# Key blocks of a fused attention kernel: where the query scales are made, and when the last weights are asked for

## The chip, the cores and the metric

One core of one Trainium2 chip. The metric is the device time of one launch in microseconds (us), as the median of several executions. The engines are TensorE (PE: matmuls and transposes; PEld: its weight loads), VectorE (DVE), ScalarE (ACT), GpSimd (POOL) and SyncE (SP, which here only issues DMAs). Each runs its own list of instructions in order and waits on semaphores for the others.

## The reference, cut to what matters

The whole block is attention with a paged cache, a second causal attention, a subject-dependent linear map and a feed-forward part with low-rank experts, for 64 sequences of 32 tokens. Only the head of the first attention bears on the change:

```
q = einsum('bsd,ed->bse', x, Wq)      # 32 heads of 128
k = einsum('bsd,ed->bse', x, Wk)      # 8 heads of 128
v = einsum('bsd,ed->bse', x, Wv)
q = rope(rmsnorm(q, q_norm_w), pos)   # rmsnorm: t * rsqrt(mean(t*t) + EPS) * w
k = rope(rmsnorm(k, k_norm_w), pos)
scores = einsum('bqhd,bkhd->bhqk', q, k_all) * SCALE
probs = softmax(where(valid, scores, -1e30))
```

`k_all` and `v_all` are the pages of a cache in front of the new keys and values. The kernel rotates queries without their norm and multiplies the scores by it later: it keeps the sums of squares of all queries and makes from them one table of **query scales** (`q_scale`), which the scores of the second stage need.

## The kernel before

Stage 1 (`stage1`) projects x with 12 blocks of weights of 512 columns: block 0 is the first half of V, blocks 1 to 8 are the queries, blocks 9 and 10 the keys, block 11 the second half of V. Every matrix is split in a high and a low part and every product is three fp32r matmuls. Stage 2 (`stage2`) is the attention over the cache; further stages follow. Between stage 1 and stage 2 stands a point that all engines must reach.

Stage 1 is written by hand, engine by engine. What follows is its key part, which runs over 16 **units** r = 0 to 15, eight for each block (`cb` = 0, 1; `u` = 0 to 7), each two tiles of 128 tokens.

- **PE** (`project`, `turn`): projections run two units ahead. In a loop it projects unit r + 2 and then transposes unit r (`turn`, L710). Unit n's projection waits until DVE has read the projection of unit n - 2 (`proj_free`), since there are two pairs of PSUM banks; `turn(r)` waits for `rotated`. After key unit 15 come the V units ("values"), the first two of them inside the same loop. From the third on they wait for `v_copied`.
- **ACT** (`k_block`): for each unit it squares the unit that has just been projected (`squares_of`, L370), takes the root of the sums (`root_of`, L377), copies what PE transposed into `turned` (`turn_copy`, L386), and in units 0 to 3 makes one quarter of the next weights' high part (`split`, L361). The two units ahead of the loop are done in front of it: squares of 0, squares of 1, then root of 0, root of 1. Behind unit 0's pieces stands `q_root` (L435), the root of all query sums, 512 columns.
- **DVE** (`rotate`, `norm`): for unit r two products with the sine and cosine tables (L585, L589; they free the banks), six small steps of the norm (L565 to L574), which need `root_of`, an addition (L596) and a multiplication by the norm (L600). In units 1 to 4 of a block a quarter of the weights' low part follows (L493). In the first block, behind units 2 to 7, stands one of six steps of `q_norm` each (L609 to L623, 512 columns), which turn `q_root` into the scales. The tiles `q_root`, `q_mean`, `q_inv` and `q_step` lie in the second quarter of `k_pool`, the place of the cache's keys, so that this quarter can't be loaded before they have been used.
- **POOL**: sixteen small copies from `q_inv` into `q_scale` (L327), then the loads of the first queries and keys of stage 2 (L70, L74), then a wait for the whole key pool and `gather_k` (L84, sixteen copies), which picks the pages of sequence 0.
- **SP** (`k_block`): asks for weights (`next_w`, L241; 1 MB), stores each unit's `turned` to `kT` (L273), and loads the key pool in 32 pieces of 256 KB (`load_pool`, L234). For the first block it asks for block 10's weights at its start, and loads two pieces behind each store. For the second block it first asks for block 11's weights, then waits for `q_scale_done` before the first store and loads two pieces behind the stores of units 1 to 4. Behind the stores of the first four V units (L248) stand two pieces each.

Of the kernel before, what the change touches and what calls it, by code (L numbers as in the profile page):

```python
# [28 lines left out]
ACT = mybir.ActivationFunctionType  # L29
# [6 lines left out]
D, HQ, HK = 128, 32, 8  # L36
G = HQ // HK
# [4 lines left out]
SEQ = P // S  # L42
NT = 4
# [46 lines left out]
def stage1(nc, c, a, scratch):  # L90

    UN = TILES // 2
    VU = UN
    RU = 2 * UN
    QM = HK * NT * G
    QN = HK * NT
    POOL_PIECES = 8
    with ExitStack() as opened:  # L98
        hold = opened.enter_context

        k_pool = c["k_pool"]
# [84 lines left out]
        pos_f = early[:, 1152:1152 + TILES]  # L186
        NQ = HK * TILES * G
        q_sums = sums[:, 0:HK, :].rearrange("p h n -> p (h n)")
        q_root = k_pool[:, quarter:quarter + NQ]
        q_mean = k_pool[:, quarter + NQ:quarter + 2 * NQ]  # L190
        q_inv = k_pool[:, quarter + 2 * NQ:quarter + 3 * NQ]
        q_step = k_pool[:, quarter + 3 * NQ:quarter + 4 * NQ]

        @block.sync
        def _(sp):
# [33 lines left out]
            def load_pool(part, piece, pieces):  # L229

                size = quarter // pieces
                first = part * quarter + piece * size
                cols = slice(first, first + size)
                sp.dma_start(k_pool[:, cols], a["kpool"][:, cols]).then_inc(c["pool_loaded"], 16)  # L234

            def next_w(blk):
                if isinstance(blk, int) and blk == 0:
                    sp.wait_ge(w_lo_piece, KC)
                else:
                    sp.wait_ge(w_lo_done, blk)  # L240
                sp.dma_start(w_raw[:, :], a["w1"][bass.ds(blk + 1, 1)].rearrange("o p n -> p (o n)")).then_inc(w_loaded, 16)  # L241
# [16 lines left out]

            def k_block(cb):

                next_w(9 + cb)
                if cb == 0:
                    for k in range(2):
                        sp.wait_ge(q_store_free[k], 16 + 16 * HK * NT // 2)
                    sp.wait_ge(q_sums_done, QN + 2)
                else:
                    sp.wait_ge(q_scale_done, SEQ * G)
                for u in range(UN):
                    b0 = u * 2 * SEQ
                    sp.wait_ge(turned_done, cb * UN + u + 3)  # L270
                    src = turned[:, u % 2, :].rearrange("p (b n) -> p b n", n=GS)
                    dst = scratch["kT"][b0:b0 + 2 * SEQ, :, cb, :].rearrange("b p n -> p b n")
                    sp.dma_start(dst, src).then_inc(store_free[u % 2], 16)  # L273
                    if cb == 0:
                        for k in range(2):
                            load_pool(u // 4 * 3, u % 4 * 2 + k, POOL_PIECES)
                    elif 1 <= u <= 4:
                        for k in range(2):
                            load_pool(1, 2 * u - 2 + k, POOL_PIECES)

            next_w(0)
            for u in range(UN):
# [16 lines left out]
        @block.gpsimd  # L299
        def _(pool):  # L300

            pool.memset(c["ident"][:, :], 0.0).then_inc(ident_step, 1)
            for s in range(SEQ):
                pool.wait_ge(ident_step, s + 1)
                pool.iota(c["tok_i"][s * S:(s + 1) * S, :], pattern=[[0, 1]], base=0, channel_multiplier=1).then_inc(ident_step, 1)
            pool.wait_ge(ident_step, SEQ + 1)
            pool.iota(key_i[:, :], pattern=[[1, L]], base=0, channel_multiplier=0).then_inc(ident_step, 1)
            pool.wait_ge(ident_step, SEQ + 2)
            pool.affine_select(out=c["ident"][:, :], in_=c["ident"][:, :], compare_op=ALU.not_equal, fill=1.0,
                               base=0, pattern=[[-1, P]], channel_multiplier=1).then_inc(ident_step, 1)  # L310
            pool.memset(ones[:, :], 1.0).then_inc(ident_step, 1)

            pool.sem_inc(q_sums_kept, 1)
            kept = q_sums.rearrange("p (h b) -> p h b", h=HK)
            with pool.Fori(0, 4) as i:
                for cb in range(2):
                    for span in range(NT):
                        pool.wait_ge(q_sums_turned, (i * 2 + cb) * NT + span + 1)
                        pool.tensor_copy(kept[:, bass.ds(i * 2 + cb, 1), span * BS:(span + 1) * BS].rearrange("p o b -> p (o b)"),
                                         sums_rows.rearrange("p (b s) -> p b s", s=S)[:, :, 0]).then_inc(q_sums_kept, 1)  # L320

            pool.wait_ge(q_inv_done, 1)
            inv4 = q_inv.rearrange("p (e h b) -> p h e b", e=2, h=SEQ)
            scale4 = c["q_scale"][:, :, :].rearrange("p b (e g) -> p g e b", g=G)
            for g in range(G):
                for q in range(SEQ):
                    pool.tensor_copy(scale4[q * S:(q + 1) * S, g, :, :], inv4[g * S:(g + 1) * S, q, :, :]).then_inc(q_scale_done, 1)  # L327

            pool.wait_ge(turn_done, RU + 2)
            pool.wait_ge(store_free[0], 16 + 16 * (VU + (RU - UN) // 2 + 1))  # L330
            for k in range(2):
                pool.wait_ge(q_store_free[k], 16 + 16 * HK * NT // 2)
            c["load_q"](pool, 0, 0)
            c["load_k_own"](pool, 0, 0)
            c["load_q"](pool, 1, 1)
            pool.wait_ge(c["pool_loaded"], 16 * 4 * POOL_PIECES)
            c["gather_k"](pool, 0, 0)

        @block.scalar
        def _(act):  # L340
# [48 lines left out]
            def v_copy(n, u, stores):  # L389

                act.wait_ge(proj_done, n + 1)
                act.wait_ge(store_free[u % 2], stores * 16 + 16)
                for t in range(2):
                    m = act.activation(turned[:, u % 2, t * 512:(t + 1) * 512], ps_proj[:, u % 2, t, :], ACT.Copy)
                m.then_inc(v_copied, 1)
# [25 lines left out]
            def k_block(cb):  # L421
                for u in range(UN):
                    r = cb * UN + u
                    ahead = cb + (u + 2) // UN
                    if not (cb == 1 and u >= UN - 2):
                        squares_of(r + 2, HK + ahead, (u + 2) % UN)
                        root_of(ahead, (u + 2) % UN)
                    if r == 0:
                        act.wait_ge(q_sums_kept, QN + 1)
                    turn_copy(r, VU + cb * (UN // 2) + u // 2, u)  # L430
                    if u < KC:
                        split(cb, 10 + cb, u)
                    if r == 0:
                        act.wait_ge(q_rotated, QM + 2)
                        act.activation(q_root, q_sums, ACT.Sqrt, bias=eps[:, 0:1], scale=1.0 / D).then_inc(q_root_done, 1)  # L435

            x_high_piece(0)
            for q in range(KC):
# [20 lines left out]
                    q_block(i, cb)  # L459
            for u in range(2):  # L460
                squares_of(u, HK, u)
            for u in range(2):
                root_of(0, u)
            for cb in range(2):
                k_block(cb)
            for u in range(UN):
                v_copy(VU + RU + u, u, VU + RU // 2 + u // 2 * 2)

        @block.vector
        def _(dve):  # L470
# [134 lines left out]
            def q_norm(k):  # L605

                if k == 0:
                    dve.wait_ge(q_root_done, 1)
                    dve.tensor_scalar(q_mean, q_sums, 1.0 / D, EPS, ALU.mult, ALU.add).then_inc(q_inv_step, 1)  # L609
                elif k == 1:  # L610
                    dve.reciprocal(q_inv, q_root).then_inc(q_inv_step, 1)
                elif k == 2:
                    dve.wait_ge(q_inv_step, 2)
                    dve.tensor_tensor(q_step, q_inv, q_inv, ALU.mult).then_inc(q_inv_step, 1)
                elif k == 3:
                    dve.wait_ge(q_inv_step, 3)
                    dve.tensor_tensor(q_step, q_step, q_mean, ALU.mult).then_inc(q_inv_step, 1)
                elif k == 4:
                    dve.wait_ge(q_inv_step, 4)
                    dve.tensor_scalar(q_step, q_step, 0.5 * SCALE, -1.5 * SCALE, ALU.mult, ALU.add).then_inc(q_inv_step, 1)  # L620
                elif k == 5:
                    dve.wait_ge(q_inv_step, 5)
                    dve.tensor_tensor(q_inv, q_step, q_inv, ALU.mult).then_inc(q_inv_done, 1)  # L623
# [40 lines left out]
            for cb in range(2):  # L664
                for u in range(UN):
                    rotate(cb * UN + u, u, tab_k, (cb, u))
                    if 1 <= u <= KC:
                        split(10 + cb, cb, u - 1)
                    if cb == 0 and 2 <= u:
                        q_norm(u - 2)  # L670

        @block.tensor
        def _(pe):
# [1350 lines left out]
```

## Time and profile before

| | us |
|---|---|
| median of 3 runs | 3061.29 |
| lowest, highest | 3060.76, 3063.66 |
| the profiled execution | 3071.46 |
| its span, from first to last instruction | 3069.9 |
| PE busy in the span | 3027.6 (99%) |
| DVE, ACT, POOL busy | 1860.2, 1543.4, 595.0 |

The profiled execution is 10.2 us longer than the median of the runs. Times within the trace are microseconds from the start of its span. On the time line a row gives start, duration, engine, line of the kernel, operation, what is written and read, how often, and in brackets how long the engine stood idle before it and what released it. Matmuls overlap, so a matmul's duration is longer than its distance to the next.

### The profile page before, as it was taken

The numbers are of one execution on the slowest core, as the hardware profiler recorded it, in microseconds if no ns is written. First come the engines' busy times: TensorE is split into PE (matmuls) and PEld (weight loads), VectorE is DVE, ScalarE is ACT, GpSimd is POOL, SyncE is SP. The second block draws the span as 40 slices with busy tenths as digits, with TensorE's granted clock in tenths as the row PEclk, the third lists the DMA queues.
The fourth block names the chain that finished last, engine by engine and source line by source line (L and its number), as shares of the span: only waits on it lengthen the run. The fifth ranks groups of instructions, "written<-read, shape, count | busy, mean of one in ns | idle before, by whom it ended". The sixth has DMA issues, their size and how long they took to land.

```text
span 3069.9 us, 91713 instructions
## 1 busy us (share of the span) xinstructions
PE 3027.6 (99%) x36256; PEld 2351.8 (77%) x36256; DVE 1860.2 (61%) x3587; ACT 1543.4 (50%) x2949; POOL 595.0 (19%) x1430
## 2 busy tenths in 40 slices
PE   8999998999999999999999999999999999999999
PEld 7777777767777777777777888888888888888887
DVE  6777768477888877888886444442333333544445
ACT  6666655377777777777776222221333333322221
POOL 0000001055455455455452000000000000200000
PEclk9999999999999999999999999999999999999999
DMA  5333334566676676676677344412333333743311
GB/s 167 97 110 105 115 110 131 166 208 205 211 220 204 206 219 206 210 220 205 209 219 229 110 126 125 124 65 100 104 103 104 97 110 100 240 148 110 109 41 55
DMA packets 508661, 456.02 MB, mean 149 GB/s; under 512 B 33985, under 2 KB 470593, under 8 KB 503746
## 3 DMA queue, kind: packets, MB, share of 16 engines
q1 hardware_dynamic: 475010, 362.80, 39.3%
q0 software_dynamic: 33344, 88.46, 8.9%
q8 instruction: 273, 4.47, 0.6%
q14 instruction: 34, 0.28, 0.0%
HBM read 321.03 MB, written 130.02 MB: 147 GB/s over the span
## 4 chain that ended last, share of the span: by engine, by line
PE 78%; DMA 1%; issue 0%; DVE 0%; ACT 0%; DVEq 0%; SPq 0%
PE ps_o L1009 18%; PE ps_scores L993 16%; PE s_ps L58 8%; PE s_ps L60 8%; PE s_ps L59 8%; PE s_ps_proj L58 5%; PE s_ps_proj L59 5%; PE s_ps_proj L60 5%; PE s_ps_o L1542 1%; PE s_ps_scores L1518 1%; PE yv_ps L60 1%; PE yv_ps L59 1%; PE yv_ps L58 1%; PE s_ps L1717 0%; PE s_ps L1708 0%
## 5 line engine op out<-in xcount | busy, mean ns | idle before, releaser
L1009 PEld LDWEIGHTS ps_o<-weights_t,v_all 32*128 32x128 f32 x17408 | 514.0, 187 | 111.1 <-issue 110.3
L1009 PE MATMUL ps_o<-weights_t,v_all 32*128 32x128 f32 x17408 | 564.4, 277 | 5.6 <-issue 3.7
L993 PE MATMUL ps_scores<-k_slot,q_slot 128*32 128x288 f32 (+1 forms) x8192 | 525.9, 397 | 7.0 <-PEq L98 4.8
L898 ACT ACTIVATE probs<-masked,shift 128x544 f32<-128x544 f32 x512 | 382.9, 748 | 248.1 <-DVE shift L944 246.6
L944 DVE CUSTOM_DVE_ANT_0 masked<-ps_scores,reach,scale_now 128x544 f32<-128x544 f32 x512 | 390.2, 762 | 179.2 <-PE ps_scores L993 175.0
L993 PEld LDWEIGHTS ps_scores<-k_slot,q_slot 128*32 128x32 f32 x8192 | 241.2, 110 | 201.6 <-issue 9.6
L957 DVE STREAM_TRANSPOSE weights_t<-probs 128x544 f32<-128x544 f32 x512 | 376.8, 736 | 23.5 <-ACT probs L903 10.3
L903 ACT ACTIVATE probs<-probs,inv 128x544 f32<-128x544 f32 x512 | 375.7, 734 | 0.0
L1101 ACT ACTIVATE s_h_hi<-s_h_raw 128x2048 fp32r<-128x2048 f32 x64 | 122.8, 1919 | 488.2 <-PE s_ps L60 472.3
L84 POOL COPY k_slot<-k_pool 128x256 f32 x1024 | 359.3, 410 | 34.8 <-DMA k_pool<-kpool_in 19.1
L58 PE MATMUL s_ps_proj<-y_hi,s_w_hi 128*128 128x512 f32 x640 | 253.1, 395 | 0.0
L59 PE MATMUL s_ps_proj<-y_lo,s_w_hi 128*128 128x512 f32 x640 | 250.0, 391 | 0.0
L60 PE MATMUL s_ps_proj<-y_hi,s_w_lo 128*128 128x512 f32 x640 | 249.1, 389 | 0.0
L58 PE MATMUL ps_proj<-x_hi,w_hi 128*128 128x512 f32 x512 | 202.9, 396 | 0.0
L414 ACT ACTIVATE turning<-ps_proj 64x512 f32<-64x512 f32 x256 | 151.8, 593 | 99.6 <-PE ps_proj L60 97.3
L58 PE MATMUL s_ps<-s_w_hi,s_h_hi 128*128 128x512 f32 x512 | 199.5, 390 | 1.4 <-DVE s_h_lo L1128 1.4
L60 PE MATMUL ps_proj<-x_hi,w_lo 128*128 128x512 f32 x512 | 199.4, 390 | 0.0
L58 PE MATMUL s_ps<-s_h_hi,s_w_hi 128*128 128x512 f32 x512 | 199.4, 389 | 0.0
L59 PE MATMUL ps_proj<-x_lo,w_hi 128*128 128x512 f32 x512 | 199.3, 389 | 0.0
L59 PE MATMUL s_ps<-s_w_lo,s_h_hi 128*128 128x512 f32 x512 | 199.2, 389 | 0.0
L60 PE MATMUL s_ps<-s_h_hi,s_w_lo 128*128 128x512 f32 x512 | 199.2, 389 | 0.0
L60 PE MATMUL s_ps<-s_w_hi,s_h_lo 128*128 128x512 f32 x512 | 199.2, 389 | 0.0
(201 smaller groups left out, 4723.0 us busy)
## 6 DMA issues: line engine op xcount, KB each, us to landing
v_all<-vpool_in SPq DMA_DIRECT2D x1024, 128.0 KB, 3.0
qT_scratch<-k_pool SPq DMA_DIRECT2D x32, 1024.0 KB, 5.1
q_slot<-qT_scratch POOLq DMA_DIRECT2D x64, 512.0 KB, 3.5
oT_scratch<-o_t POOLq DMA_DIRECT2D x128, 256.0 KB, 5.1
s_h_raw<-oT_scratch SPq DMA_DIRECT2D x32, 1024.0 KB, 5.8
aT_scratch<-s_o_t SPq DMA_DIRECT2D x32, 1024.0 KB, 5.7
s_h_raw<-aT_scratch SPq DMA_DIRECT2D x32, 1024.0 KB
w_raw<-w_in SPq DMA_DIRECT2D x11, 1024.0 KB, 8.0
```

The costliest lines, as they stand in the source:

```text
L58: pe.matmul(out, a_hi, b_hi, start=start, stop=False)
L59: pe.matmul(out, a_hi, b_lo, start=False, stop=False)
L60: return pe.matmul(out, a_lo, b_hi, start=False, stop=stop)
L84: m = pool.tensor_copy(k_slots[slot][:, first + k, :], k_pool[:, bass.ds(page[k], 1), :].rearrange("p o n -> p (o n)"))
L414: act.activation(swapped[g][to, :], bank[g][of, :], ACT.Copy)
L898: act.activation(probs[:, k % BUF, :], masked[:, k % 2, :], ACT.Exp, bias=shift[:, k % BUF:k % BUF + 1], scale=-1.0, accum_out=total[:, k ...
L903: act.activation(probs[:, k % BUF, :], probs[:, k % BUF, :], ACT.Copy, scale=inv[:, k % BUF:k % BUF + 1]).then_inc(w_done, 1)
L944: dve.tensor_tensor_reduce(masked[:, k % 2, :], ps_scores[:, k % 2, LOW:LOW + KEYS], reach[:, k // HK, :], scale_now[:, k // HK, k % HK:k ...
L957: dve.transpose(weights_t[:, k // G % 4, k % G, :], probs[:, k % BUF, :]).then_inc(turned_w, 1)
L993: m = pe.matmul(ps_scores[q * S:(q + 1) * S, k % 2, cols], q_slots[j][:, head, r * S:(r + 1) * S], k_slots[j][:, pages, head * PSIZE:(head ...
L1009: m = pe.matmul(ps_o[:, q, 0:GS], v_all[rows, j, t, e * D:(e + 1) * D], weights_t[rows, g, :, t * S:(t + 1) * S], start=t == 0, stop=t == NPP)
L1101: act.activation(h_hi[k % 2][:, :, :].rearrange("p g (b s) -> p b g s", s=S), h_raw[k % 2][:, :, :].rearrange("p b (g s) -> p b g s", s=S) ...
```

## The change

Four things are altered, all in stage 1.

1. ACT takes the root of key unit 0 right behind its squares, ahead of the squares of unit 1.
2. The query scales are made later. `q_root` moves on ACT from behind key unit 0 to behind the second V unit's copy, the six `q_norm` steps on DVE from between the key units to behind all of them, and the sixteen copies on POOL from ahead of the three first loads of stage 2 to behind them. The four tiles move from `k_pool` into `by_cos` and `by_sin`, the rotation's tiles, which are not used any more by then. A wait for the copies is added before `gather_k`.
3. SP asks for block 11's weights behind the sixth store of the first key block and its two pieces, where before it did so behind the eighth. SP no longer waits for the scales.
4. The second quarter of the key pool is loaded in the second key block one piece behind each of the eight stores, where before it was two pieces behind stores 1 to 4.

```
-        q_root = k_pool[:, quarter:quarter + NQ]
...
+        q_root, q_mean = by_cos[:, 0:NQ], by_cos[:, NQ:2 * NQ]
+        q_inv, q_step = by_sin[:, 0:NQ], by_sin[:, NQ:2 * NQ]
...
             def k_block(cb):
 
-                next_w(9 + cb)
                 if cb == 0:
+                    next_w(9)
...
-                else:
-                    sp.wait_ge(q_scale_done, SEQ * G)
...
                             load_pool(u // 4 * 3, u % 4 * 2 + k, POOL_PIECES)
-                    elif 1 <= u <= 4:
-                        for k in range(2):
-                            load_pool(1, 2 * u - 2 + k, POOL_PIECES)
+                        if u == 5:
+                            next_w(10)
+                    else:
+                        load_pool(1, u, POOL_PIECES)
...
+            pool.wait_ge(q_inv_done, 1)
...
+                    pool.tensor_copy(scale4[q * S:(q + 1) * S, g, :, :], inv4[g * S:(g + 1) * S, q, :, :]).then_inc(q_scale_done, 1)
+
+            pool.wait_ge(q_scale_done, SEQ * G)
             pool.wait_ge(c["pool_loaded"], 16 * 4 * POOL_PIECES)
             c["gather_k"](pool, 0, 0)
...
             for u in range(2):
                 squares_of(u, HK, u)
-            for u in range(2):
                 root_of(0, u)
...
                 v_copy(VU + RU + u, u, VU + RU // 2 + u // 2 * 2)
+                if u == 1:
+                    act.wait_ge(rotated, RU + 1)
+                    act.activation(q_root, q_sums, ACT.Sqrt, bias=eps[:, 0:1], scale=1.0 / D).then_inc(q_root_done, 1)
...
-                    if cb == 0 and 2 <= u:
-                        q_norm(u - 2)
+            for k in range(UN - 2):
+                q_norm(k)
```

**ACT, at the head of the key units** (`squares` x8 is one unit; `k_pool<-sums,eps` is `q_root`). Before:

```order
L370 ACTIVATE squares,sums<-ps_proj 128x128 x16
L377 ACT_TABLE_LOAD
L377 ACTIVATE root<-sums,eps 128x8 x2
L370 ACTIVATE squares,sums<-ps_proj 128x128 x8
L377 ACTIVATE root<-sums,eps 128x8
L386 ACTIVATE turned<-ps_turn 128x4x4x32 x2
L361 ACTIVATE w_hi<-w_raw 128x512
L435 ACTIVATE k_pool<-sums,eps 128x512
```

Now:

```order
L368 ACTIVATE squares,sums<-ps_proj 128x128 x8
L375 ACT_TABLE_LOAD
L375 ACTIVATE root<-sums,eps 128x8
L368 ACTIVATE squares,sums<-ps_proj 128x128 x8
L375 ACTIVATE root<-sums,eps 128x8
L368 ACTIVATE squares,sums<-ps_proj 128x128 x8
L375 ACTIVATE root<-sums,eps 128x8
L384 ACTIVATE turned<-ps_turn 128x4x4x32 x2
L359 ACTIVATE w_hi<-w_raw 128x512
```

The table load and the first root stand between the squares of unit 0 and of unit 1, and `q_root` is gone from here.

**DVE, from the end of key unit 4 to the products of unit 5** (L611 is the longest of the six `q_norm` steps). Before:

```order
L596 TENSOR_TENSOR turning<-by_cos,by_sin 128x1024
L600 TENSOR_TENSOR turning<-turning,nw 128x1024
L493 TENSOR_TENSOR w_lo<-w_raw,w_hi 128x512
L611 RECIPROCAL k_pool<-k_pool 128x512
L585 TENSOR_TENSOR by_cos<-ps_proj,k_pool 128x1024
L589 TENSOR_TENSOR by_sin<-ps_proj,k_pool 128x8x64 x2
```

Now, behind the last key unit:

```order
L597 TENSOR_TENSOR turning<-turning,nw 128x1024
L606 TENSOR_SCALAR by_cos<-sums 128x512
L608 RECIPROCAL by_sin<-by_cos 128x512
L611 TENSOR_TENSOR by_sin<-by_sin 128x512
L614 TENSOR_TENSOR by_sin<-by_sin,by_cos 128x512
L617 TENSOR_SCALAR by_sin<-by_sin 128x512
L620 TENSOR_TENSOR by_sin<-by_sin 128x512
L98 UNCONDITIONAL_BRANCH
```

All six steps stand in a row there, and nothing but the end of the stage follows.

**SP, from the last stores of the first key block into the second** (`kT_scratch` is a unit's store, `k_pool<-kpool_in` a piece of the pool). Before, from the store of unit 7:

```order
L273 DMA kT_scratch<-turned 128x8x128 [waits turned_done]
L234 DMA k_pool<-kpool_in 128x512 x2
L241 DMA w_raw<-w_in 128x2048 [waits w_lo_done]
L273 DMA kT_scratch<-turned 128x8x128 [waits turned_done,q_scale_done]
L273 DMA kT_scratch<-turned 128x8x128 [waits turned_done]
L234 DMA k_pool<-kpool_in 128x512 x2
```

Now, from the store of unit 5:

```order
L269 DMA kT_scratch<-turned 128x8x128 [waits turned_done]
L232 DMA k_pool<-kpool_in 128x512 x2
L239 DMA w_raw<-w_in 128x2048 [waits w_lo_done]
L269 DMA kT_scratch<-turned 128x8x128 [waits turned_done]
L232 DMA k_pool<-kpool_in 128x512 x2
L269 DMA kT_scratch<-turned 128x8x128 [waits turned_done]
L232 DMA k_pool<-kpool_in 128x512 x2
L269 DMA kT_scratch<-turned 128x8x128 [waits turned_done]
L232 DMA k_pool<-kpool_in 128x512
```

The request for the weights stands two stores earlier, and every store of the second block has one piece behind it.

## Rows read from the trace of the kernel before

**Rows 1.** Busy us (x instructions) by stretch, granted clock, DMA share, GB/s
```profile
463.02:575.87 112.85, 102.75 (x481) 84.70 (x481) 98.37 (x181) 54.17 (x277) 8.50 (x16) 0.94 0.46 136
617.10:3069.90 2452.80, 2437.99 (x33536) 1894.62 (x33536) 1442.13 (x2903) 1193.65 (x2152) 562.27 (x1350) 1.00 0.51 154
```
**Rows 2.** Time line of PE: transposes (L710), first matmuls behind a gap
```profile
465.26 1.97 PE L710 MATMUL ps_turn<-ident,turning 128*128 128x128 f32 x8 [2.08 <-DVE turning L600]
475.34 1.03 PE L710 MATMUL ps_turn<-ident,turning 128*128 128x128 f32 x8
488.56 1.04 PE L710 MATMUL ps_turn<-ident,turning 128*128 128x128 f32 x8
492.62 0.79 PE L58 MATMUL ps_proj<-w_hi,x_hi 128*128 128x512 f32 x1 [3.03 <-DVE by_sin L589]
499.77 1.03 PE L710 MATMUL ps_turn<-ident,turning 128*128 128x128 f32 x8
531.46 1.03 PE L710 MATMUL ps_turn<-ident,turning 128*128 128x128 f32 x8
536.70 0.61 PE L58 MATMUL ps_proj<-w_hi,x_hi 128*128 128x512 f32 x1 [4.20 <-DVE by_sin L589]
575.87 1.03 PE L710 MATMUL ps_turn<-ident,turning 128*128 128x128 f32 x8
579.06 0.50 PE L58 MATMUL ps_proj<-w_hi,x_hi 128*128 128x512 f32 x1 [2.15 <-ACT turned L394]
617.12 5.24 PE L993 MATMUL ps_scores<-k_slot,q_slot 128*32 128x288 f32 x44 [4.75 <-PEq L98]
```
**Rows 3.** Time line of ACT, 453 to 585 us
```profile
453.04 0.25 ACT L370 ACTIVATION_READ_ACCUMULATOR squares<-ps_proj 128x1 f32 x1
459.97 1.28 ACT L377 ACT_TABLE_LOAD   x1
461.27 0.49 ACT L377 ACTIVATE root<-sums,eps 128x8 f32<-128x8 f32 x2
492.12 0.63 ACT L361 ACTIVATE w_hi<-w_raw 128x512 fp32r<-128x512 f32 x1
532.96 0.63 ACT L361 ACTIVATE w_hi<-w_raw 128x512 fp32r<-128x512 f32 x1 [4.16 <-DMA w_raw<-w_in]
583.69 1.09 ACT L394 ACTIVATE turned<-ps_proj 128x512 f32<-128x512 f32 x2 [4.68 <-DMA kT_scratch<-turned]
```
**Rows 4.** Time line of DVE, 461 to 562 us
```profile
461.60 0.17 DVE L565 TENSOR_SCALAR nw<-sums 128x8 f32<-128x8 f32 x1 [5.81 <-ACT root L377]
486.95 3.35 DVE L611 RECIPROCAL k_pool<-k_pool 128x512 f32<-128x512 f32 x1
534.23 1.22 DVE L585 TENSOR_TENSOR by_cos<-ps_proj,k_pool 128x1024 f32<-128x1024 f32 x1
548.69 1.22 DVE L585 TENSOR_TENSOR by_cos<-ps_proj,k_pool 128x1024 f32<-128x1024 f32 x1
555.14 1.22 DVE L585 TENSOR_TENSOR by_cos<-ps_proj,k_pool 128x1024 f32<-128x1024 f32 x1
561.17 1.23 DVE L585 TENSOR_TENSOR by_cos<-ps_proj,k_pool 128x1024 f32<-128x1024 f32 x1
```
**Rows 5.** SP's time line; then us to landing, stores issued at 528.9, 553.9, 571.7
```profile
524.74 0.47 SPq L241 DMA_DIRECT2D w_raw<-w_in  x1
...
kT_scratch<-turned SPq DMA_DIRECT2D x1, 512.0 KB, 5.6
...
kT_scratch<-turned SPq DMA_DIRECT2D x1, 512.0 KB, 3.5
...
kT_scratch<-turned SPq DMA_DIRECT2D x1, 512.0 KB, 3.2
```
**Rows 6.** Time line of POOL: the scale copies, and the first gather
```profile
516.41 9.37 POOL L327 COPY q_scale<-k_pool 32x128 f32<-32x128 f32 x16 [63.18 <-DVE k_pool L623]
598.18 5.54 POOL L84 COPY k_slot<-k_pool 128x256 f32 x16 [19.09 <-DMA k_pool<-kpool_in]
```

More of the change, by code:

```diff
@@ L188, in stage1 @@
         q_sums = sums[:, 0:HK, :].rearrange("p h n -> p (h n)")
-        q_root = k_pool[:, quarter:quarter + NQ]
-        q_mean = k_pool[:, quarter + NQ:quarter + 2 * NQ]
-        q_inv = k_pool[:, quarter + 2 * NQ:quarter + 3 * NQ]
-        q_step = k_pool[:, quarter + 3 * NQ:quarter + 4 * NQ]
+        q_root, q_mean = by_cos[:, 0:NQ], by_cos[:, NQ:2 * NQ]
+        q_inv, q_step = by_sin[:, 0:NQ], by_sin[:, NQ:2 * NQ]
         @block.sync
@@ L320, in _ @@
                                          sums_rows.rearrange("p (b s) -> p b s", s=S)[:, :, 0]).then_inc(q_sums_kept, 1)
[L322 to L327, printed above, removed]
             pool.wait_ge(turn_done, RU + 2)
@@ L335, in _ @@
             c["load_q"](pool, 1, 1)
+            pool.wait_ge(q_inv_done, 1)
+            inv4 = q_inv.rearrange("p (e h b) -> p h e b", e=2, h=SEQ)
+            scale4 = c["q_scale"][:, :, :].rearrange("p b (e g) -> p g e b", g=G)
+            for g in range(G):
+                for q in range(SEQ):
+                    pool.tensor_copy(scale4[q * S:(q + 1) * S, g, :, :], inv4[g * S:(g + 1) * S, q, :, :]).then_inc(q_scale_done, 1)
+            pool.wait_ge(q_scale_done, SEQ * G)
             pool.wait_ge(c["pool_loaded"], 16 * 4 * POOL_PIECES)
@@ L432, in k_block @@
                         split(cb, 10 + cb, u)
-                    if r == 0:
-                        act.wait_ge(q_rotated, QM + 2)
-                        act.activation(q_root, q_sums, ACT.Sqrt, bias=eps[:, 0:1], scale=1.0 / D).then_inc(q_root_done, 1)
             x_high_piece(0)
```

## The prediction

> **What bounds the kernel now.** I read the busy time by stretch first, then PE's time line, then those of the engines that PE waits for. Stage 2 and all that follows is PE at work for 2437.99 of 2452.80 us at a granted clock of 1.00 [rows 1]; nothing in the change reaches there. The key units are another matter: in their 112.85 us PE is busy for 102.75, DVE for 98.37, and the granted clock is 0.94 [rows 1]. So the reading is of this stretch alone, and of the 41 us behind it up to the start of stage 2 at 617.12 [rows 2].
>
> PE's rhythm there is one projection and one group of eight transposes per unit. Undisturbed, that period is 6.34 us: from the transposes of unit 4 at 499.77 to those of unit 9 at 531.46 it is 31.69 us for five [rows 2]. Every departure from it is a loss. PE stands ready for the transposes of unit 0 at 463.2 (465.26 less the idle 2.08), and starts those of unit 15 at 575.87 [rows 2]. That is 112.7 us for fifteen periods, which undisturbed are 95.1. **17.6 us are lost**, in three places [rows 2]:
> - Units 0 and 1: 2.1 us of idle time before unit 0's transposes, and 475.34 - 465.26 - 6.34 = 3.7. The eight transposes take 1.97 us, where those of later units take 1.03: TensorE is at its lower clock (1.2 of 2.4 GHz) behind the wait. Together 5.8.
> - Units 1 to 4: 488.56 - 475.34 - 2 x 6.34 = 0.5, and 499.77 - 488.56 - 6.34 = 4.9, with an idle 3.03 before the projection at 492.62 whose first matmul is 0.79 long; the clock is down again. Together 5.4.
> - Units 9 to 15: 575.87 - 531.46 - 6 x 6.34 = 6.4, with an idle 4.20 before the projection at 536.70.
>
> **Part 1, the first root.** DVE stands idle for 5.81 us until 461.60, because the root of unit 0 waits behind unit 1's squares [rows 4]. ACT had unit 0's squares at 453.29 and then waited for unit 1's projection; the table load of 1.28 us and both roots (0.49) come at 459.97 [rows 3]. Now table load and root stand at 453.3 and are done by about 455.3, which is ahead of unit 1's squares: nothing on ACT comes later. Unit 0 was turned at 465.26, 3.7 us behind the norm's start at 461.60; the norm now starts when DVE has done the products, 5.8 us sooner (461.60 less 5.81), so unit 0 is rotated near 459.5, ahead of 463.2, when PE is ready. The idle 2.1 goes, with it the low clock. Unit 1's products can start at 460.0 (its squares are done just before the table load of 459.97 [rows 3]) and free the banks 2.47 us later: the products at 534.23 let PE start at 536.70 [rows 2, 4]. That is 462.5, in time. All 5.8 us go.
>
> **Part 2, the scales out of the key units.** The reciprocal alone keeps DVE for 3.35 us right before the products of unit 5, for which PE waits [rows 4]. Without the six steps DVE's period is 6.03 us (555.14 to 561.17), or 6.45 with a piece of the weights' low part (548.69 to 555.14) [rows 4]. The first is under PE's 6.34. The second is over it by 0.11, and occurs at four units of each block. So the 5.4 us go, but DVE becomes what is late next, narrowly. A piece of the high part on ACT ends at 492.12 + 0.63, that is 4.19 us behind the transposes at 488.56 [rows 2, 3]. With 0.6 for the low part and 2.47 for the products, PE is free to go on 7.3 us behind them; by its own rhythm it wants to go on at 6.34 + 0.9 = 7.24, where 0.9 is 6.34 less the 5.4 us of a projection. That is 0.1 us for the first piece and 0.1 for each of the next three, 0.4 per block, **0.8 us back**. The bounds are 0 (DVE's slack absorbs it, as it does partly in the last six periods) and 2.
>
> Where the six steps and the copies go there must be cover. `q_root` can run when the second V unit has been copied: 583.69 + 1.09 [rows 3], shifted by the gain to about 568.3. None of the rows has it in that place; two copies of the same 512 columns take 1.09, which bounds it. ACT then has its next unit to wait for, and PE's next is two units behind. On DVE the reciprocal is 3.35, and each of the other five steps is at most 1.23, the price of 1024 columns [rows 4]: 9.5 at most. The sixteen copies are 9.37 and the gather 5.54 [rows 6]. So the chain ends by 568.3 + 1.1 + 9.5 + 9.4 + 5.5 = 593.8 at the latest. Stage 2 starts at 617.12 less the gain, 600.6. **The chain has 6.8 us to spare and costs nothing.** Before it was the last piece of the pool that started the gather at 598.18 [rows 6]; that piece is now at 581.7, ahead of the copies' end.
>
> **Part 3, the last weights.** ACT waits 4.16 us for the weights of block 11 until 532.96 and DVE and PE behind it [rows 2, 3]; they had been asked for at 524.74 [rows 5], 8.2 us earlier. Now the request stands two stores earlier. In the new rhythm unit 5 is turned at 463.2 + 0.4 + 31.7 = 495.3, its store follows about 3.7 us later (ACT squares unit 7 in between), two pieces follow, and the request is out at 501.5: the weights land at 509.7. ACT wants them 3.56 us (492.12 - 488.56) behind the transposes of unit 8, at 518. The wait goes with 8 us in hand, and with it 6.1 us of the 6.4; the other 0.3 is DVE's lateness, counted above.
>
> The request now stands ahead of unit 6's store. That store has a twin: the one at 528.9 was issued 4.1 us behind such a request and took 5.6 us to land, against 3.5 with two pieces behind it and no such load ahead [rows 5]. Its buffer is wanted again two units later, 11 us after the issue. It costs nothing. The Trainium skill ("DMA: Bandwidth & Descriptors", section "Queues, rings and completion order") says that the increment of a DMA's semaphore lands only after every earlier write from the same SDMA engine, across queues. This speaks against the new place, and the 5.6 us agree with it. By the rule the store lands no sooner than the weights, some 4 us after its issue, and the sum is the same.
>
> **Part 4, one piece per unit.** SP has time: in the key units a piece is asked for in under a microsecond and a unit lasts 6.34. The one place where it can hurt is behind unit 15's store, where there was no piece. ACT's second V copy waits for that store, until 583.69, and PE's fourth V projection waits for the copy [rows 3]. A store with nothing behind it landed in 3.2 us, one with two pieces in 3.5 [rows 5]: **0.3 us back**. The upper bound is 2.4 (5.6 less 3.2), if the piece acts as the 1 MB load did; nothing suggests a gain. I take 0.3, since a piece behind a store is what the 3.5 shows.
>
> **The sum.** 5.8 + 5.4 + 6.4 = 17.6 gained, 0.8 + 0.3 given back: 16.5 us. The profiled execution of 3071.46 us would take 3055.0, its span 3053.4 instead of 3069.9. The median of the runs is 10.2 us under the profiled one; the gain is taken off it whole: 3061.29 - 16.5 = **3044.8 us**, 0.54% less.
>
> **Rivals.**
> - *The V units give some of it back.* The third waits 2.15 us for ACT, as before [rows 2]. The additional piece delays the stores behind it, on which ACT's next two copies wait; at its upper bound that is 2.4 us, and if TensorE falls to its lower clock in the longer wait, the following unit takes 7.15 us (492.62 to 499.77) instead of 5.4 [rows 2], 1.8 more. The gain is 12.6 to 15, the time near 3048. Against it: the first matmul behind the 2.15 is only 0.50 long, not 0.79 [rows 2], so the clock held there. The Trainium skill ("TensorE: Matmul & The Clock Gate", section "What's actually happening") calls the throttled clock the default, which activity lifts; the wait of 2.08 that ended at 465.26 was followed by the lower clock and that of 2.15 was not [rows 2], so the trace bears the rule out at one of two waits of like length, and by the rule a wait that was harmless before need not stay so. 0.14.
> - *The last weights still hold up a unit,* because load and stores hamper each other more than the twin shows. It decides from 8 us of further delay, and gives the 6.1 us back: 3050.9. 0.06.
> - *The scales' chain ends stage 1, and the kernel is slower.* The chain from `q_root` to the end of the gather is 25.5 us in series at its bounds, at the very end of the stage, where before only the gather stood. It sets the start of stage 2 from 6.8 us over that price on, and makes the kernel slower from 6.8 + 16.5 = 23.3 us on, that is if steps on DVE and POOL took about twice as long there. At two and a third times the price the time is near 3072. For it speaks that POOL's durations are rough; against it that DVE has nothing else to do then, and that the 9.37 us were measured beside a busy DVE. Late but not slower 0.03, slower 0.03.
> - *The change doesn't do what it says:* other waits stand right behind those removed, and the time is within 6 us of the old. Nothing in the rhythm of units 4 to 9 shows one. 0.02.
>
> **How the numbers follow.** The forecast has a chance of 0.72; with the others that is 1. About 0.2% (6 us) is what a measurement of this kernel can tell from no change. Faster by more: 0.72 + 0.14 + 0.06 + 0.03 = 0.95; same 0.02; slower 0.03. The range: at the best neither the 0.8 nor the 0.3 is given back, 3043.7, and runs spread by a microsecond or two, so 3042. Upwards it takes in DVE's bound and the V units' case to 12.6 (3048.7) and the same spread: 3050.
>
> **What would show it.** In the changed trace: the transposes of unit 0 near 463.2 and 1.03 long; those of unit 15 near 559 and no idle time over 0.3 on PE between; DVE never over 1 us idle up to unit 8; the third V unit still waiting about 2.1; ACT's second V copy at 567.3; the scale copies on POOL over by 589, the gather by 594, both ahead of PE's last V matmul near 595; stage 2 from 600.6. A wait for weights near 518, a first V matmul of 0.79, or a stage 2 that starts right behind the gather would each show its rival right. The sum would be wrong if the period of 6.34 us did not hold for fifteen units in a row: DVE would then be at a wait that the gaps of before had hidden.

## The result

| | us |
|---|---|
| before, median of 6 runs | 3061.38 (3060.76 to 3065.18) |
| changed, median of 6 runs | 3048.30 (3045.06 to 3052.43) |
| ratio | 0.9955 (0.9945 to 0.9965) |
| the changed kernel's profiled execution | 3048.38, span 3046.8 |

The ratio is the changed kernel's time over that of the kernel before in the same comparison, with its 95% interval in brackets. The change makes the kernel 13.1 us faster, where 16.5 were forecast. 16.5 us are a ratio of 0.9946, inside the interval, near its lower end. The changed kernel's runs lie on about 3045, 3048 and 3052; the profiled execution is a middle one. The trace of before that the prediction used was a long one: 3071.46 where its median is 3061.

The stretches of the changed kernel, us (from:to, length, busy PE, PEld, DVE, ACT, POOL, granted clock, DMA share, GB/s):

```profile
463.02:559.30 96.28, 96.28 (x484) 80.36 (x482) 87.09 (x166) 53.48 (x276) 0.00 (x0) 1.00 0.53 156
559.30:600.00 40.70, 33.89 (x151) 27.38 (x149) 6.24 (x8) 10.35 (x20) 14.14 (x35) 0.99 0.60 204
600.00:3046.80 2446.80, 2433.48 (x33536) 1891.27 (x33536) 1445.70 (x2904) 1193.29 (x2152) 561.56 (x1350) 1.00 0.51 155
```

The key units, 112.85 us in [rows 1], now take 96.28, with PE busy for all of them and the clock at 1.00. PE's time line there, with the start of stage 2:

```profile
462.87 1.04 PE L707 MATMUL ps_turn<-ident,turning 128*128 128x128 f32 x8
469.23 1.03 PE L707 MATMUL ps_turn<-ident,turning 128*128 128x128 f32 x8
475.75 1.03 PE L707 MATMUL ps_turn<-ident,turning 128*128 128x128 f32 x8
...
520.43 1.03 PE L707 MATMUL ps_turn<-ident,turning 128*128 128x128 f32 x8
527.01 1.03 PE L707 MATMUL ps_turn<-ident,turning 128*128 128x128 f32 x8
...
559.01 1.03 PE L707 MATMUL ps_turn<-ident,turning 128*128 128x128 f32 x8
562.20 0.50 PE L58 MATMUL ps_proj<-w_hi,x_hi 128*128 128x512 f32 x1 [2.15 <-ACT turned L392]
600.05 7.88 PE L990 MATMUL ps_scores<-k_slot,q_slot 128*32 128x288 f32 x80 [4.71 <-PEq L98]
```

Against [rows 2] the idle times of 2.08, 3.03 and 4.20 are gone, the 2.15 in the V units stays. From unit 0 to unit 15, fifteen periods, it takes 96.1 us. Stage 2 starts at 600.05 instead of 617.12, **17.07 us** sooner. The next rows are ACT's first root, and its later `q_root` with the copies around that:

```profile
453.14 1.28 ACT L375 ACT_TABLE_LOAD   x1
454.44 0.30 ACT L375 ACTIVATE root<-sums,eps 128x8 f32<-128x8 f32 x1
...
566.72 1.08 ACT L392 ACTIVATE turned<-ps_proj 128x512 f32<-128x512 f32 x2 [4.57 <-DMA kT_scratch<-turned]
567.69 0.72 ACT L464 ACTIVATE by_cos<-sums,eps 128x512 f32<-128x512 f32 x1
570.32 1.09 ACT L392 ACTIVATE turned<-ps_proj 128x512 f32<-128x512 f32 x2 [1.91 <-DMA v_pages_scratch<-turned]
```

And the scales' chain on DVE (its first and last step) and POOL:

```profile
568.44 0.43 DVE L606 TENSOR_SCALAR by_cos<-sums 128x512 f32<-128x512 f32 x1 [12.16 <-ACT by_cos L464]
...
574.08 0.69 DVE L620 TENSOR_TENSOR by_sin<-by_sin 128x512 f32<-128x512 f32 x1
...
574.84 7.60 POOL L331 COPY q_scale<-by_sin 32x128 f32<-32x128 f32 x16 [12.60 <-DVE by_sin L620]
583.44 5.54 POOL L84 COPY k_slot<-k_pool 128x256 f32 x16 [1.00 <-POOL q_scale L331]
```

The chain is over at 588.98, 11.1 us ahead of stage 2. So the trace puts 17 us into stage 1, the timed runs show 13, and the two profiled spans differ by 23.1. The experiments had to say which of these is the change's.

### The profile page after: what moved, and what is told of

Same layout as the page of the kernel before. It is cut to its first block, busy times and chain, and to the rows that moved or that the text cites. A ratio compares the mean times of both kernels' runs of the same rounds, so it can differ in the third digit from the quotient of the medians.

```text
span 3046.8 us, 91713 instructions
## 1 busy us (share of the span) xinstructions
PE 3016.6 (99%) x36256; PEld 2344.2 (77%) x36256; DVE 1863.7 (61%) x3587; ACT 1543.1 (51%) x2949; POOL 592.6 (19%) x1430
## 4 chain that ended last, share of the span: by engine, by line
PE 79%; issue 0%; DVE 0%; ACT 0%; DMA 0%; DVEq 0%
PE ps_o L1006 18%; PE ps_scores L990 16%; PE s_ps L58 8%; PE s_ps L60 8%; PE s_ps L59 8%; PE s_ps_proj L58 5%; PE s_ps_proj L59 5%; PE s_ps_proj L60 5%; PE s_ps_o L1539 1%; PE s_ps_scores L1515 1%; PE yv_ps L60 1%; PE yv_ps L59 1%; PE yv_ps L58 1%; PE s_ps L1714 0%; PE s_ps L1705 0%
```

## The experiments

Each is the kernel before or the changed one with one edit, or with none. The kernel before was run beside them each time, and every ratio is against it. Where two ratios are set against each other below, they come from the same comparison, unless it is said otherwise. 0.001 of the time is 3.1 us.

**The kernel before again.** No edit.

> The kernel before, unchanged, to see how much of a launch's time is not set by the code. The trace of before spans 3069.9 us, its timed runs lie near 3061; the trace of after spans 3046.8 and its timed runs fall on 3045, 3048 and 3052. Theory A: the key units are the same in every execution (unit 0 turned at 465.3, unit 15 at 575.9, stage 2 from 617.1), and what differs lies behind 617, above all at the end of stage 2, where the trace of before has 98 matmuls in 5.91 us at the lower clock and that of after in 3.16. Then the span here is 3060 to 3070 with stage 2 from 617. Theory B: the low clock in the key units is itself a matter of the execution, and stage 2 starts up to 4 us earlier here than in the first trace.

Measured: 3061.68 (10 runs; ratio 1.0001, 0.9989 to 1.0012), profiled span 3060.2. Stage 2 started at 615.1, not 617.1, so there is truth in theory B. From there to the start of the third stage it took 1057.0 us against 1063.0 in the first trace, as theory A has it. Both scatter. In stage 1 the two executions differ most at the gap for the last weights; unit 0 and the period behind it are 0.3 and 0.6 us later here. The projection behind the gap, in the first trace and in this one:

```profile
536.70:543.86 7.16, 7.16 (x24) 5.69 (x25) 6.85 (x17) 0.77 (x2) 0.00 (x0) 0.76 0.50 146
```
```profile
536.35:541.93 5.58, 5.58 (x24) 4.56 (x25) 5.38 (x11) 0.78 (x2) 0.00 (x0) 1.00 0.63 188
```

Here the same 24 matmuls ran at a granted clock of 1.00 behind a gap of 3.02, and the load landed in 7.0 us, not 8.2. The period from unit 9 to unit 10 was 9.65 instead of 12.40: over the undisturbed 6.34, this loss is 3.3 us in one execution and 6.1 in another.

**Only the first root.**

```
-            for u in range(2):
                 root_of(0, u)
```

> Only the first root is moved (part 1). The prediction's sum gives it 5.8 us: the idle 2.1 before unit 0's transposes and the 3.7 behind it go, the later losses stay at 5.4 and 6.4. Stage 2 from 611.3, time 0.9981 of before. Rival: the time comes back at the next wait (DVE's six steps and the wait for weights absorb it), and stage 2 starts within 1 us of 617.1.

Measured: 3055.21 (10 runs), ratio 0.9982 (0.9970 to 0.9994), as expected. In its trace unit 9 is turned at 526.39, 5.9 us ahead of the kernel before in the run above (532.28). But stage 2 starts at 612.7, only 2.4 ahead, because the gap for the weights was 4.00 long, with the low clock behind it:

```profile
531.43:539.50 8.07, 8.07 (x25) 6.35 (x26) 7.69 (x19) 0.79 (x2) 0.00 (x0) 0.67 0.44 130
```

Unit 10 came 13.11 us behind unit 9, a loss of 6.8, the largest in any trace. The traced execution was a long one, 3061.52. Against the first trace it starts stage 2 4.4 us sooner, so the rival, less than 1 us, is not met either way; the ten timed runs carry the verdict.

**Only the scales.** The edit is part 2 of the change with the SP wait gone, and nothing else.

> Only the query scales are moved (part 2), with the wait of SP for them gone; first root, request for the last weights and pairs of pieces as before. The sum gives 5.4 us less: stage 2 from 611.7, time 0.9982 of before. The transposes of unit 4 come 13.2 us, not 18.6, ahead of those of unit 6 less the periods. Rival: the gap at unit 4 was due to the lateness carried over from units 0 and 1, and only part of the 5.4 goes.

Measured: 3058.75 (10 runs), ratio 0.9991 (0.9981 to 1.0001), half of what was expected and not clear of nothing. In the trace the step is as forecast: units 2, 3 and 4 are 6.58 and 6.39 us apart, where in the repeated run of before they are 6.88 and 11.22. The rival, that this loss was carried over from units 0 and 1, falls: those are as late here as ever (10.98 us apart). Again the period at the later gap is longer than in the repeated run of before (11.62 against 9.65), and stage 2 starts at 612.7.

**Only the last weights.**

```
-                next_w(9 + cb)
...
+                        if u == 5:
+                            next_w(10)
```

> Only the request for the last weights is moved behind the sixth store (part 3). The sum gives 6.1 us less: the idle 4.20 before the projection at 536.70 goes and with it the low clock behind it; stage 2 from 611.0, time 0.9980 of before. Rival: less than 4 us, if in some executions of before the clock doesn't fall in that gap.

Measured: 3058.22 (10 runs), ratio 0.9988 (0.9978 to 0.9998). The period at the gap is 6.57 and stage 2 starts at 611.7, 3.4 us sooner than in the repeated run of before and 5.4 sooner than in the first. The timed gain is 3 to 4 us, the rival's, and its condition was met in the repeated run of before. The interval, 0.6 to 6.7 us, does not exclude the 6.1. Added up, the three single edits bring 12.0 us timed.

**The changed kernel again.** No edit.

> The changed kernel, unchanged, to see which part of its 13 us in the timed runs is fixed and which varies. Theory: stage 1 has no clock lottery left, so the transposes of units 0 and 15 and the start of stage 2 fall within 0.5 us of 462.9, 559.0 and 600.05 of its first trace, while stage 2 and behind scatter by several us as in before. Against before, whose stage 2 started at 617.1 and 615.1 in two traces, that is 15 to 17 us; ratio 0.9945 to 0.996. Rival: stage 2 itself has become longer by 2 to 4 us, which would show in its span (1063.0 and 1057.0 in before, 1058.5 in after).

Measured: 3047.05 (6 runs), ratio 0.9943 (0.9929 to 0.9956), slightly under what was expected. In this comparison the medians are 16.4 us apart, in the first they were 13.1. The key units are the same to 0.1 us in length, but unit 0 is already 0.8 later, and with it unit 15, and stage 2 starts at 602.34. The theory was wrong on that: a part that varies from execution to execution is left, in the V units and ahead of the key units.

```profile
563.10 0.60 PE L58 MATMUL ps_proj<-w_hi,x_hi 128*128 128x512 f32 x1 [2.16 <-ACT turned L392]
602.34 6.51 PE L990 MATMUL ps_scores<-k_slot,q_slot 128*32 128x288 f32 x64 [4.72 <-PEq L98]
```
```profile
563.10:567.00 3.90, 3.90 (x10) 3.08 (x11) 0.00 (x0) 0.00 (x0) 0.04 (x1) 0.56 0.94 294
```

Behind the same wait for ACT (2.15 and 2.16 us) the clock held in one execution and fell to 0.56 for 3.9 us in the other. From unit 15's transposes to stage 2 it was 41.04 us in the first, 42.43 in the second. Stage 2 took 1058.3 us here and 1058.5 in the first trace, between the 1057.0 and 1063.0 of before. No lengthening of 2 to 4 us shows, which speaks against the rival; with two traces of each, one us would not be seen.

**The changed kernel with the late request for the weights.**

```
                 if cb == 0:
-                    next_w(9)
...
+                next_w(9 + cb)
```

> The changed kernel with the request for the last weights back at the start of the second block. Theory: a gap of 3 to 4 us before the projection behind unit 9's transposes, with 0 to 2.8 us of low clock behind it, by how long the load takes (7.0 to 8.2 us so far) and how soon the clock falls; stage 2 from 603.4 to 606.5, 0.1 to 0.2% slower than the changed kernel. Rival: under 1 us, if the scales were what made the request late.

Measured: 3052.93 (6 runs), ratio 0.9965 (0.9952 to 0.9978) against the changed kernel's 0.9943: 0.0022 or 6.7 us, though the two intervals overlap. Stage 2 starts at 604.65, 4.6 us later than in the first trace of the changed kernel, within what was expected. A gap of 2.94 us came back, with the lower clock behind it:

```profile
520.45 1.03 PE L705 MATMUL ps_turn<-ident,turning 128*128 128x128 f32 x8
524.43 0.79 PE L58 MATMUL ps_proj<-w_hi,x_hi 128*128 128x512 f32 x1 [2.94 <-DVE by_sin L584]
531.42 1.04 PE L705 MATMUL ps_turn<-ident,turning 128*128 128x128 f32 x8
```

**The changed kernel with the first roots late.**

```
             for u in range(2):
                 squares_of(u, HK, u)
+            for u in range(2):
                 root_of(0, u)
```

> The changed kernel with both first roots behind both squares again (part 1 undone). Theory: the idle 2.1 before unit 0's transposes and the lower clock behind it come back: unit 0 near 465.5, unit 1 10.0 to 11.0 us later, everything from unit 2 on in the undisturbed rhythm, stage 2 5.5 to 7.5 us later than in the changed kernel, 605.6 to 607.5. Rival: DVE, which is the late engine in units 1 to 5 of the changed kernel, hides a part, and it is under 4.

Measured: 3052.64 (9 runs), ratio 0.9969 (0.9959 to 0.9979), where the pairs variant below, practically the changed kernel, had 0.9954: 4.6 us, with overlapping intervals. Units 0 and 1 are 10.91 us apart, much as in before (10.63 in the repeated run), and stage 2 starts at 609.2, 9.1 us later than in the first trace of the changed kernel. That is later than expected. 7.7 of it are there at unit 15, of which 0.6 came from unit 0, which was that much later than in the repeated run of before; 1.4 came when the clock fell in the V units too (42.5 us behind unit 15). The trace speaks against the rival, under 4.

**The changed kernel with the pool in pairs.**

```
-                    else:
-                        load_pool(1, u, POOL_PIECES)
+                    elif 1 <= u <= 4:
+                        for k in range(2):
+                            load_pool(1, 2 * u - 2 + k, POOL_PIECES)
```

> The changed kernel with the second quarter of the pool loaded in pairs behind the stores of units 1 to 4 of the second block, as before (part 4 undone). Theory: nothing stands behind unit 15's store, so it lands 0.1 to 0.3 us sooner than the 5.4 of the changed kernel, and the fourth V projection follows the third without a gap (0.2 in one trace of the changed kernel); stage 2 starts within 0.5 us of that of the changed kernel in an execution whose clock holds in the V units (41.0 us behind unit 15's transposes). Rival of the prediction, that the piece costs up to 2.4 us: stage 2 2 us earlier.

Measured: 3047.61 (4 runs), ratio 0.9954 (0.9938 to 0.9971). Stage 2 starts at 600.04, in the changed kernel at 600.05; unit 15's store lands in 5.4 us in both, where 0.1 to 0.3 less was expected. In the traces the fourth part of the change costs and brings nothing.

**The scale copies four times over.** The values are the same. Each copy but the first also waits for the one before, which costs nothing: one copy takes 0.48 us, as in the changed kernel.

```
+            for again in range(4):
...
+                        if again or g or q:
+                            pool.wait_ge(q_scale_done, again * SEQ * G + g * SEQ + q)
...
+            pool.wait_ge(q_scale_done, 4 * SEQ * G)
```

> The changed kernel with the sixteen copies into q_scale made four times over (the same values again), so that the chain of the scales is longer by three times 7.6 us = 22.8. In the changed kernel the gather ended at 588.98 and stage 2 began at 600.05. Theory: the chain has 10 to 11 us to spare, then sets the start: gather over at about 611.8, stage 2 from about 612.5, 12 us later than in the changed kernel. Rival: PE's start waits for the gather only and engines do not meet at that point for POOL, in which case stage 2 starts at 600 and its first scores wait.

Measured: one run, 3056.19. POOL's time line:

```profile
574.50 30.46 POOL L334 COPY q_scale<-by_sin 32x128 f32<-32x128 f32 x64 [12.91 <-DVE by_sin L623]
605.95 5.53 POOL L84 COPY k_slot<-k_pool 128x256 f32 x16 [0.99 <-POOL q_scale L334]
```

The gather ends at 611.48 and stage 2 starts at 612.23, as expected: the engines meet behind POOL too. So the third rival's mechanism, a chain that sets the start of stage 2, is real. The gather came 0.75 us ahead of stage 2 here and 11.1 ahead in the changed kernel, so that takes some 10 us of delay.

**Two edits in the V units, apart and together.** `v_first` lets ACT copy the first V unit before unit 15's transposes (the first lines below); `late_loads` puts POOL's three first loads behind the wait for DVE's six steps (the second).

```
                     r = cb * UN + u
+                    if r == RU - 1:
+                        v_copy(VU + RU, 0, VU + RU // 2)
...
-                v_copy(VU + RU + u, u, VU + RU // 2 + u // 2 * 2)
+                if u:
+                    v_copy(VU + RU + u, u, VU + RU // 2 + u // 2 * 2)
```

```
+            pool.wait_ge(q_inv_done, 1)
             c["load_q"](pool, 0, 0)
             c["load_k_own"](pool, 0, 0)
             c["load_q"](pool, 1, 1)
-            pool.wait_ge(q_inv_done, 1)
```

> The changed kernel with POOL's three first loads of stage 2 behind the six steps on DVE, and nothing else. Theory: unit 15's store, which took 5.4 us beside these loads, lands in 3.6; ACT's second V copy runs 1.8 us earlier, but PE gains nothing, since the third V projection still starts 2.15 late and ends after that copy. Stage 2 41.0 us behind unit 15's transposes, as in the changed kernel.

> The changed kernel with ACT copying the first V unit before unit 15's transposes, and nothing else. Theory: the idle 2.15 before the third V projection goes, but the fourth now waits about 2.0 for the second V copy, which waits for unit 15's store (5.4 us beside POOL's loads); stage 2 40.5 to 41 us behind unit 15's transposes. Both edits are needed for the 2 us of the version that has both (39.2 us).

> A version meant to beat both: ACT copies the first V unit before it copies unit 15's transposes, and POOL issues the first loads of stage 2 behind the six steps on DVE, so that unit 15's store does not share the DMA engines with them. Theory: the idle 2.15 before the third V projection goes; unit 15's store lands in 3.5 us instead of 5.5, so the fourth V projection waits under 0.5. Stage 2 from 598.0, 2 us earlier, which the timed runs can hardly tell (ratio to before 0.0007 lower than the changed kernel's). Rival: the wait only moves to the fourth V projection, and the gain is under 0.5.

Measured: `late_loads` 3051.29 and `v_first` 3048.90, one run each; both together 3043.22 (6 runs), ratio 0.9937 (0.9922 to 0.9951) beside the changed kernel's 0.9943. PE's gap in the V units, with `v_first` alone and with both:

```profile
568.64 0.50 PE L58 MATMUL ps_proj<-w_hi,x_hi 128*128 128x512 f32 x1 [2.57 <-ACT turned L392]
```
```profile
565.33 0.50 PE L58 MATMUL ps_proj<-w_hi,x_hi 128*128 128x512 f32 x1 [0.48 <-ACT turned L392]
...
597.53 4.65 PE L993 MATMUL ps_scores<-k_slot,q_slot 128*32 128x288 f32 x48 [4.71 <-PEq L98]
```

Alone, `v_first` moves the wait from the third projection to the fourth (2.57), since the second V copy waits for unit 15's store, which takes 5.7 us beside POOL's loads. Alone, `late_loads` makes that store land in 3.6 and PE gains nothing. In both the clock fell behind the gap, and stage 2 came 42.9 and 42.4 us behind unit 15, where 40.5 to 41 and 41.0 were expected. Together the gap is 0.48 and stage 2 comes 39.2 us behind unit 15, where it was 41.04 in the changed kernel with the clock held: the two edits bring 1.9 us. Stage 2 starts at 597.53, 2.5 us ahead of the changed kernel; the other 0.6 is there at unit 15 already, from an execution that came to the key units earlier. In the timed medians it is 3.8 us with overlapping intervals. So the trace shows a gain and the ratio doesn't prove it.

## Why the prediction was right, and where it was not

The measured 3048.3 lies in the range of 3042 to 3050, 3.5 us over the forecast. The mechanism was right: three waits in the key units, each with its own cause, and all three are gone. By the prediction's own steps:

- **The first root, 5.8.** Right. Alone it brings 0.9982, and taking it away from the change costs 0.0015 (5.5 and 4.6 us timed). In five traces with the late root the wait and the period behind it lose 5.8 to 6.7 us. Table load and root were over at 454.7 (forecast 455.3) and unit 0 was turned at 462.87, at the full clock.
- **The scales, 5.4.** Right in the traces: the idle 3.03 and the period of 11.21 are gone, and all four traces that still have the six steps between the key units lose 5.4 us or more at units 1 to 4. Timed alone it brought only 0.9991 (up to 0.9981). Of three parts it has the poorest match, and its interval reaches 5.8. No run took this part out of the changed kernel; whether the 5.4 is whole in an average execution stays open.
- **DVE late next, 0.8 back.** Right: fifteen periods are 96.1 us, 1.0 over 95.1, at the eight units named (for instance 469.23 to 475.75, 6.52, and 520.43 to 527.01, 6.58). Its sum for the first piece was rounded up: 4.19 + 0.6 + 2.47 = 7.26 is 0.02 over 7.24, not 0.1. The trace has about 0.2 there.
- **The last weights, 6.1 of the 6.4.** The mechanism was right; the size is not a fixed one. It came from one execution, in which the load took 8.2 us and the projection behind the gap ran at a clock of 0.76. Five traces have the late request: before, its repeat, `root_only`, `scales_only` and the changed kernel with the late request. They lose 6.1, 3.3, 6.8, 5.3 and 4.6 us there, 5.2 in the mean. Timed, the edit alone brought 3.7 us (0.9988), and taking it out of the change cost 6.7. So 6.1 is on the high side of the mean and neither shown nor excluded as an average; the term should have had its own range. The request stood at 501.01 (forecast 501.5).
- **The store behind the request.** It landed in 4.8 us; its twin's 5.6 was 4.3 in the repeated run of before. In all fourteen traces such a store lands 1.4 to 2.7 us behind the weights asked for ahead of it (in the changed kernel 509.9 and 508.3). That agrees with the rule of the Trainium skill ("DMA: Bandwidth & Descriptors", section "Queues, rings and completion order") that the prediction names. It is a weak test: with the 3.5 us of a store that has no such load ahead, most of them would have landed behind the weights too (508.6 here).
- **One piece per unit, 0.3 back.** It costs 0.0. The prediction took the wrong store as its base. The 3.2 us in [rows 5] are unit 14's store. Unit 15's, for which ACT's second V copy waits, was issued at 578.0 in that trace and took 5.6 us, beside POOL's first loads (577.2 to 579.1). It takes 5.4 in the changed kernel and 3.6 with `late_loads`, so it is those loads that count and not the piece. The 2.4 us of delay in the first rival come from the same reading.
- **The scales' chain.** Forecast at the latest 593.8, measured 588.98; it has 11.1 us to spare, not 6.8. The copies take 7.60 us with DVE idle and took 9.37 beside its rotations [rows 6].
- **The first rival, at 0.14,** was too low. Its first half, a later store, did not come (5.4 us for unit 15's, 5.6 in before). Its second half did: the clock in the V units fell in 4 of the 8 traced executions of the changed kernel and its variants with a gap of over 2 us there. Where the gap was 2.15, that cost 1.4 us each time. In the five executions of before and of its single edits it held; whether the change makes the fall more likely, or this is chance, stays open. The argument against the rival was poor: a first matmul of 0.50 does not show that the clock holds. `v_first` has 0.50 and then 0.63 from the fifth matmul on.

All of it together is read from the start of stage 2: 617.1 and 615.1 in before, 600.05 and 602.34 in the changed kernel. The means differ by 14.9 us, 0.49%; the two ratios, 0.9955 and 0.9943, have 0.45 and 0.57%. The forecast of 0.54% lies between them. That the first pair of traces gives 17.07, so near the 16.5, is partly luck: it pairs an execution of before that lost 6.1 us at the weights with one of the changed kernel whose clock held in the V units. And taking the gain of a long execution off the median whole leans to the high side, since 2 of the 10.2 us by which that execution was long lay in stage 1, and stage 1 is where the gain was read. The 23.1 between the profiled spans is 17.1 from stage 1; the other 6.0 is the first trace of before, whose stage 2 was 4.5 us longer than the changed kernel's. 2.75 of that stand at its end, where the same 98 matmuls take 5.91 us and 3.16 in the changed kernel:

```profile
1674.27 5.91 PE L1009 MATMUL ps_o<-weights_t,v_all 32*128 32x128 f32 x98 [1.80 <-issue]
```
```profile
1655.49 3.16 PE L1006 MATMUL ps_o<-weights_t,v_all 32*128 32x128 f32 x98 [1.80 <-issue]
```

The idle time ahead is 1.80 in both, and the matmuls are the same. It is not the change that sets this: the repeated run of before has 3.16 there (behind 0.70), and the pairs variant of the changed kernel has 4.61 behind the same 1.80.

## What to carry to other kernels

Where two engines share a rhythm, subtract the undisturbed period from every period. The sum of what is left is all that an edit there can bring, and each gap names its own cause. A gap costs its idle time surely and the low clock behind it sometimes: price the second as a range, or take more than one trace, since one trace can show either end. When a wait is removed, look which engine's period is the next longest. Move late work to where its engine has nothing else to do, with its whole chain added up against the next meeting point. And take the price of a transfer from the very transfer that will be waited for, with the neighbours that it has there.

## What the runs showed of the hardware

The length of a gap alone does not say whether TensorE's granted clock falls behind it. Behind 2.15 or 2.16 us in the V units it held in nine traces and fell in three, to 0.56 over 3.9 us in one of them. Behind 2.08 us before unit 0's transposes the projection that followed ran at 0.64 to 0.72 in all five traces that have this wait. Behind the gap for the last weights it fell in four of five traces (2.94 to 4.20 us long, clock 0.67 to 0.78) and held in one (3.02 us long, 1.00). Behind 1.80 at the end of stage 2 the same matmuls took 3.16, 4.61 and 5.91 us in three traces.

A store of 512 KB took 3.2 to 3.9 us in the key units with no larger load near it (traces of before, of the changed kernel and of `late_loads`). It took 4.3 to 5.6 about 4 us behind the request for 1 MB of weights on its own queue, and 5.4 to 5.7 beside POOL's loads of 1.1 MB on another queue. Sixteen small POOL copies took 9.37 us beside a busy DVE and 7.60 beside an idle one. They read another tile there, and no run separates the two, so the cause is not shown.
